# Perceiver block on one Trainium2 core: softmax sums laid on a masked square, one set of products for adding and broadcasting them

## The reference, cut to what matters

```
q = split_heads(layernorm(x) @ Wq.T + bq)       # x: 32 batches, 64 rows, 256 columns; 16 heads of 16
k = split_heads(ctx @ Wk.T + bk)                # ctx: 32 batches, 1601 keys, 256 columns
v = split_heads(ctx @ Wv.T + bv)
score = einsum('bhqd,bhkd->bhqk', q, k) * sqrt(16)
attn = softmax(score, axis=-1)
out = einsum('bhqk,bhkd->bhqd', attn, v)
x = x + out @ Wp.T + bp
x = x + circuit_block(layernorm(x))             # cosines, running products, a small two-layer network
x = x + experts(layernorm(x))                   # a shared expert and two of seven routed ones
```

## Time and profile before

| what | us |
|---|---|
| median of 3 runs (1733.7 to 1734.82) | 1734.32 |
| the profiled execution | 1735.91 |
| its span, first to last instruction | 1734.1 |
| attention, its 64 `weigh` blocks: first and last start | 83.9, 1209.1 |

### The profile page before, as it was taken

The page is one execution under the profiler, slowest core; times in us unless marked ns, Lnnn a source line. Parts: engine busy times, 40 slices in busy tenths (PEclk is TensorE's granted clock), DMA queues, the critical chain, the costliest instruction groups (busy, mean ns, idle before and its releaser), DMA issues. The chain is left out here.

```text
span 1734.1 us, 59228 instructions
## 1 busy us (share of the span) xinstructions
PE 1666.1 (96%) x24340; PEld 1377.8 (79%) x24340; DVE 1425.4 (82%) x3316; ACT 1220.5 (70%) x3297; POOL 948.8 (55%) x1427
## 2 busy tenths in 40 slices
PE   7999999999999999999999999996798899999998
PEld 4777777777777777777777777775577899999998
DVE  5699898998989989898998989888875676767657
ACT  3687788777888778887877878787554365656552
POOL 5265646556465565655556555554310448888850
PEclk9999999999999999999999999996797999999999
DMA  5011111211112111121111111111102356666632
GB/s 177 22 64 46 48 66 42 67 45 53 60 42 68 45 63 50 42 68 45 65 48 45 65 46 64 48 48 57 62 25 86 122 177 228 219 228 219 226 120 103
DMA packets 43439, 147.89 MB, mean 85 GB/s; under 512 B 5680, under 2 KB 25008, under 8 KB 39712
## 3 DMA queue, kind: packets, MB, share of 16 engines
q1 hardware_dynamic: 38416, 130.72, 22.1%
q0 software_dynamic: 4752, 13.38, 2.5%
HBM read 129.79 MB, written 14.16 MB: 83 GB/s over the span
## 5 line engine op out<-in xcount | busy, mean ns | idle before, releaser
L506 ACT ACTIVATE a_probs<-a_probs,a_bias 128x401 f32<-128x401 f32 x1024 | 631.8, 622 | 2.1
L721 DVE TENSOR_SCALAR_CACHE_REDUCE a_probs<-a_pss 128x401 f32<-128x401 f32 x1024 | 526.2, 570 | 56.9 <-PE a_pss L976 42.6
L736 DVE STREAM_TRANSPOSE a_pT<-a_probs 128x1664 f32<-128x1664 f32 x256 | 488.1, 1907 | 61.3 <-PE a_pso L1005 59.8
L976 PE MATMUL a_pss<-a_keys,a_qown 32*32 32x401 f32 x8192 | 273.6, 508 | 2.7 <-issue 1.3
L316 POOL TENSOR_TENSOR a_clo<-a_raw,a_chi 128x416 fp32r<-128x416 f32 x240 | 251.5, 1081 | 0.0
L1005 PEld LDWEIGHTS a_pso<-a_pT,a_v 128*32 128x32 f32 x6656 | 184.5, 112 | 45.7 <-issue 42.8
L1005 PE MATMUL a_pso<-a_pT,a_v 128*32 128x128 f32 x6656 | 202.5, 279 | 3.5 <-ACT a_op L521 2.7
L339 POOL TENSOR_SCALAR a_ex<-a_probs,a_marks 128x4 f32<-128x4 f32 x256 | 75.9, 296 | 220.2 <-ACT a_probs L506 218.1
L1670 PE MATMUL e_psg<-e_xh,e_guh 128*128 128x256 f32 x660 | 189.5, 287 | 5.5 <-DVE e_hl L1416 4.0
L506 ACT ACTIVATION_READ_ACCUMULATOR a_probs<-a_probs,a_bias 128x1 f32 x1024 | 194.5, 190 | 0.0
L1671 PE MATMUL e_psg<-e_xl,e_guh 128*128 128x256 f32 x660 | 186.6, 283 | 0.0
(11 more groups left out here) (253 smaller groups left out, 4288.8 us busy)
## 6 DMA issues: line engine op xcount, KB each, us to landing
a_raw<-in_ctxT SPq DMA_DIRECT2D x60, 832.0 KB, 4.4
f_gur<-in_wgu SPq DMA_DIRECT2D x24, 1408.0 KB, 6.2
f_dr<-in_wd SPq DMA_DIRECT2D x24, 768.0 KB, 4.7
e_big<-ys_scr SPq DMA_DIRECT2D x8, 512.0 KB, 7.0
a_probs<-in_ctxT SPq DMA_DIRECT2D x2, 1664.0 KB, 9.3
a_x<-in_x SPq DMA_DIRECT2D x16, 128.0 KB, 4.4
rows_scr<-f_a SPq DMA_DIRECT2D x8, 256.0 KB, 2.3
rows_scr<-f_a SPq DMA_DIRECT2D x4, 512.0 KB, 3.5
```

The lines of the kernel that those rows point to most:

```text
L506: nc.scalar.activation(z, z, ACT.Exp, bias=bias[:, h % 2, at_bias:at_bias + 1], scale=-1.0, accum_out=esum[:, h % 2, j, 2 * e + r:2 * e + ...
L721: nc.vector.tensor_scalar(probs[:, at % RING, j, 0:KG], ps_s[:, j, 0:KG], -SCALE, None, ALU.mult, ALU.min, accum_out=nmax[:, h % 2, at_max ...
L736: nc.vector.transpose(pT[:, turned_slot(h, i)].rearrange("p j k -> p (j k)"), probs[:, at % RING].rearrange("p j k -> p (j k)")).then_inc( ...
L976: mm = nc.tensor.matmul(ps_s[32 * g:32 * g + 32, j, 0:KG], q_own[32 * j:32 * j + 32, n % 2, m, e, 32 * r:32 * r + 32], keys[32 * j:32 * j ...
```

## The change

The keys are dealt out differently: key i goes to group i mod 4, so that group 0 has 401 real keys and the others 400 (`REAL`). The one absent column of groups 1 to 3 is set to -1e30 once in the score banks and never written again, so its probability is 0. With that `less_extra`, `total`, `spread_sums` and `spread` are gone, and the scale in the last value copy too. In their place POOL lays the 128 by 16 sums on a masked 128 by 512 square (`lay_sums`), PE adds them over all partitions and broadcasts them in one set of four products with a matrix of ones (`totals`, behind `weigh`), DVE takes the reciprocal of the broadcast 128 by 128 bank (`invert`), and ACT's `copy_out` becomes two activations of 64 columns with the parity as scale. On PE the lone first-quarter step of an even period joins the second quarter, and the two steps of the third quarter both stand ahead of `spread_max`. In DVE's order behind the loop the last `invert` stands behind `rows.0 scan.0`.

```diff
-        plan = [[(n + 1, 2)], [(n + 1, 3), (n + 1, 4)], [(n + 1, 5), (n + 1, 6)], [(n + 1, 7), (n + 1, 8), (n + 1, 9)]]
+        plan = [[], [(n + 1, 2), (n + 1, 3), (n + 1, 4)], [(n + 1, 5), (n + 1, 6)], [(n + 1, 7), (n + 1, 8), (n + 1, 9)]]
...
-            def spread_sums(h):
-
-                pool.wait_ge(inverse_ready, h + 1)
+            def lay_sums(h):
+
+                pool.wait_ge(exp_done, HALF * HALF * (h + 1))
                 if h > 0:
 
-                    pool.wait_ge(sums_filled, h)
+                    pool.wait_ge(totals_filled, h)
...
+                nc.gpsimd.tensor_tensor(out=sums_in[:].rearrange("p j (q b) -> p (j q) b", b=32),
+                                        in0=esum[:, h % 2].rearrange("p j q -> p (j q)").unsqueeze(2).to_broadcast([P, 4 * HALF, 32]),
+                                        in1=mark[:, DIAG].unsqueeze(1).to_broadcast([P, 4 * HALF, 32]), op=ALU.mult).then_inc(sums_laid, 1)
...
                 act.wait_ge(o_filled, h + 1)
-                act.wait_ge(sums_filled, h + 1)
+                act.wait_ge(inverse_ready, h + 1)
...
-                nc.scalar.copy(o_part[:, h % 2, :], ps_o[:, 0:2 * P]).then_inc(o_copied, 1)
+                for e in range(2):
+                    last = nc.scalar.activation(o_part[:, h % 2, SQ * e:SQ * (e + 1)], ps_o[:, SQ * e:SQ * (e + 1)], ACT.Identity, scale=mark[:, e:e + 1])
+                last.then_inc(o_copied, 1)
...
             def invert(h):
 
-                dve.wait_ge(total_filled, h + 1)
-                if h > 0:
-
-                    dve.wait_ge(sums_spread, h)
-                nc.vector.reciprocal(inverse[:], ps_s[0:32, 0, W:W + 4 * HALF]).then_inc(inverse_ready, 1)
+                dve.wait_ge(totals_filled, h + 1)
+                if h > 1:
+
+                    dve.wait_ge(o_scaled, h - 1)
+                nc.vector.reciprocal(o_part[:, h % 2, P:2 * P], ps_o[:, P:2 * P]).then_inc(inverse_ready, 1)
...
+            nc.vector.memset(ps_s[:, :, min(REAL):KG], ABSENT).then_inc(absent_set, 1)
...
                     if i == 2 and h > 0:
-                        if h + 1 < NH:
-                            dve.wait_ge(s_filled, HALF * (HALF * (h + 1) + 3) + 1)
                         invert(h - 1)
...
-            def spread(h):
-
-                pe.wait_ge(sums_spread, h + 1)
+            def totals(h):
+
+                pe.wait_ge(sums_laid, h + 1)
                 for j in range(HALF):
-                    for e in range(2):
-                        mm = nc.tensor.matmul(ps_o[32 * j:32 * j + 32, P + SQ * e:P + SQ * (e + 1)], mark[0:32, PARITY[e]],
-                                              sums_in[:, j, 2 * e:2 * e + 2].rearrange("p q b -> p (q b)"), start=True, stop=True)
-                mm.then_inc(sums_filled, 1)
+                    mm = nc.tensor.matmul(ps_o[32 * j:32 * j + 32, P:2 * P], ones[:], sums_in[:, j, :], start=True, stop=True)
+                mm.then_inc(totals_filled, 1)
...
                 if h > 0:
                     weigh(h - 1)
+                    totals(h - 1)
                 for z in steps[0]:
                     step(*z)
 
-                if h > 0:
-                    total(h - 1)
                 if h + 1 < NH:
                     scores(h + 1, 3)
...
-                for z in steps[2][:1]:
+                for z in steps[2]:
                     step(*z)
+
                 if h + 1 < NH:
                     spread_max(h + 1)
-                for z in steps[2][1:]:
-                    step(*z)
-
                 if h + 2 < NH:
                     scores(h + 2, 1)
-                if h > 0:
-                    spread(h - 1)
```

More of the change, by code:

```diff
@@ L39 @@
 RING, TURNED = 6, 5
-OWN, DIAG, EXTRA, KEPT, PARITY = slice(0, 2), slice(2, 34), slice(34, 35), slice(35, 36), (slice(36, 68), slice(68, 100))
+REAL = tuple((SK + QK - 1 - g) // QK for g in range(QK))
+ABSENT = -1e30
+OWN, DIAG = slice(0, 2), slice(2, 34)
 SCALE = float(HD) ** 0.5
@@ L154, in attention_and_circuit @@
         a_id_sb = sb("a_id", [P, P])
-        mark = sb("a_marks", [P, 100])
+        mark = sb("a_marks", [P, 34])
         tick = sb("a_tick", [P, 1])
         nmax, lowest, bias = sb("a_nmax", [P, 2, HALF * HALF]), sb("a_low", [HALF * HALF, 2, 32]), sb("a_bias", [P, 2, HALF * HALF])
-        esum, extra, sums = sb("a_esum", [P, 2, HALF, 4]), sb("a_ex", [P, HALF]), sb("a_sums", [P, 2, HALF, 4])
-        sums_in = sb("a_sin", [32, HALF, 4, 32])
-        inverse, o_part = sb("a_inv", [32, HALF * 4]), sb("a_op", [P, 2, 4 * SQ])
+        esum, sums_in, ones = sb("a_esum", [P, 2, HALF, 4]), sb("a_sin", [P, HALF, P]), sb("a_ones", [P, 32])
+        o_part = sb("a_op", [P, 2, 4 * SQ])
         oT = sb("a_oT", [P, NC, P])
@@ L372, in _ @@
             nc.gpsimd.memset(unset, 0.0).then_inc(cleared, 1)
+            nc.gpsimd.memset(ones[:], 1.0).then_inc(cleared, 1)
             nc.gpsimd.memset(tick[:], 0.0).then_inc(ticked, 1)
@@ L389, in period @@
                 n, k = h // 2, h % 2
+                if h > 0:
+                    lay_sums(h - 1)
                 if h > 1:
                     gather(h - 2)
-                less_extra(h, 0)
                 if h % 4 == 1 and h > 4:
@@ L437, in _ @@
             period(NH - 3)
+            lay_sums(NH - 3)
             gather(NH - 4)
-            less_extra(NH - 2, 0)
-            less_extra(NH - 2, 1)
             pool.wait_ge(kv_filled, STEPS * B)
             nc.gpsimd.memset(expo[:], -0.5).then_inc(expo_set, 1)
-            for i in range(0, NT // 2, 4):
+            for i in range(0, NT, 4):
                 nc.gpsimd.memset(heads[:, i:i + 4, :], 0.0).then_inc(zeroed, 1)
[L445 to L449, removed]
+            lay_sums(NH - 2)
             gather(NH - 3)
-            less_extra(NH - 1, 0)
             pool.wait_ge(by_set, 6)
@@ L462, in _ @@
             nc.gpsimd.memset(c[:].rearrange("p t (h d) -> p (t h) d", d=HD)[:, :, 0], 0.0).then_inc(zeroed, 1)
[L463 to L464 removed]
+            add_bias(NT - 1)
+            lay_sums(NH - 1)
             gather(NH - 2)
[L466 to L467 removed]
             pool.wait_ge(turned, HALF * NH)
@@ L502, in exponentials @@
                 act.wait_ge(bias_ready, h + 1)
+                if i == 0 and h > 1:
+                    act.wait_ge(sums_laid, h - 1)
                 for j in some:
@@ L542, in copy_steps @@
                         else:
-                            nc.scalar.activation(v_of(n)[:, t, :], step_bank(at)[:, 0:D], ACT.Identity, scale=mark[:, KEPT]).then_inc(kv_copied, 1)
+                            nc.scalar.copy(v_of(n)[:, t, :], step_bank(at)[:, 0:D]).then_inc(kv_copied, 1)
             def copy_rows(g):
@@ L969, in scores @@
                 if at == 0:
-                    pe.wait_ge(q_ready_all, NC * NG)
+                    pe.wait_ge(absent_set, 1)
                 for j in range(HALF):
@@ L975, in scores @@
                     for g in range(QK):
-                        mm = nc.tensor.matmul(ps_s[32 * g:32 * g + 32, j, 0:KG], q_own[32 * j:32 * j + 32, n % 2, m, e, 32 * r:32 * r + 32],
-                                              keys[32 * j:32 * j + 32, m, g * KG:(g + 1) * KG], start=True, stop=True)
+                        mm = nc.tensor.matmul(ps_s[32 * g:32 * g + 32, j, 0:REAL[g]], q_own[32 * j:32 * j + 32, n % 2, m, e, 32 * r:32 * r + 32],
+                                              keys[32 * j:32 * j + 32, m, g * KG:g * KG + REAL[g]], start=True, stop=True)
                     mm.then_inc(s_filled, 1)
@@ L1066, in _ @@
             pe.wait_ge(ctx0_split, NC)
-            pe.wait_ge(cleared, 3)
+            pe.wait_ge(cleared, 4)
             for s in range(FIRST_STEPS):
@@ L1125, in _ @@
                 if stage == "weigh":
-                    total(NH - 1)
                     weigh(NH - 1)
+                    totals(NH - 1)
                     pe.wait_ge(loaded, 16 * 7)
-                    idle_work(6)
-                    spread(NH - 1)
+                    idle_work(4)
                 elif stage == "project":
@@ L1796 @@
     ctx = a["ctx_1024"]
-    ctx = np.concatenate([ctx[:, :SK - 1].reshape(B, QK, KG - 1, D), np.broadcast_to(ctx[:, None, SK - 1:], (B, QK, 1, D))], axis=2)
-    ctx = np.pad(ctx, ((0, 0), (0, 0), (0, W - KG), (0, 0))).reshape(B, QK, KT, 32, D).transpose(0, 2, 1, 3, 4).reshape(B, SKP, D)
+    ctx = np.stack([np.pad(ctx[:, g::QK], ((0, 0), (0, W - REAL[g]), (0, 0))) for g in range(QK)], axis=1)
+    ctx = ctx.reshape(B, QK, KT, 32, D).transpose(0, 2, 1, 3, 4).reshape(B, SKP, D)
     at = np.arange(P)
```

35 lines of the change are left out of this document (6 added, 29 removed), and 2 rows, old and new, of the table DVE_ORDER.

## The result

| | before | after |
|---|---|---|
| median, us | 1734.01 (4 runs, 1733.5 to 1734.82) | 1758.38 (4 runs, 1756.82 to 1758.86) |
| span of the profiled execution | 1734.1 | 1757.0 |
| first `weigh` | 83.91 | 87.29 |
| first to last `weigh` | 1125.14 | 1144.59 |
| behind the last `weigh` | 525.07 | 525.14 |

The ratio is 1.0142, with a 95% interval from 1.0128 to 1.0156: slower by some 24 us. Of the 22.9 us by which the span grew, 3.4 lie ahead of the first `weigh` and 19.5 between the first and the last, where the odd periods grew and the even ones shrank.

A forecast was written before the change was run, and what follows sets the result against it. PE was taken to be the bound, in a loop with DVE that binds odd periods. 30 x (1.03 - 0.40) = +18.9 plus 2.7 for the last reciprocals gave +21.6 and 1756 us, range 1724 to 1771.

The forecast's parts named there:

- the predicted case: Reciprocal holds DVE from 0.8 to 1.3 us and ACT's copies hold PE; 1740 to 1769 us, chance 0.68.
- the predicted loop: `weigh` releases DVE's turn; reciprocal and third take then release PE's scores of quad 0, 7.95 + R behind `weigh`'s start.
- The reciprocal: On DVE, ahead of the third take: widened from 16 to 128 columns, 234 ns becomes 1.11 us, 7.8 ns a column.
- R: Time the reciprocal holds DVE before the next take: 1.09 us predicted, against 0.19 before the change.
- Eight plain passes a column: The skill page's reading of the reciprocal on DVE: 1.29 us, R = 1.27, whole forecast 1767.
- ACT's copies: Fourth quarter: PE waits for step copies after later `spread_max` (start s), 0.75 us in odd periods, 0.24 in even.
- `totals`: On PE behind `weigh`: eight more instructions than `weigh` alone, 0.24 us with the turn to the scores.
- Even periods: `weigh` to `weigh`: 17.98 us against 18.38, -0.40; only R above 0.87 shows, costing 0.22.
- Odd periods: `weigh` to `weigh`: the loop binds, 16.96 + R = 18.05 us against 17.02, +1.03.
- Periods with `project_out`: Every fourth period, treated as the other odd ones, so +1.03 us.
- The sum: 30 even and 30 odd periods give +18.9 us, the last three reciprocals 2.7; +21.6 in all.
- A sign that failed: DVE's wait for `weigh` ahead of its second turn was to become smaller than 0.94 us.

The follow-up runs named there:

- the late reciprocal: The changed kernel with DVE's reciprocal moved from ahead of the third take to behind the fourth, before the last turn: 1736.23 us.
- the copy: The changed kernel with a plain copy of the 128 by 128 bank in place of its reciprocal, the division left out: 1738.01 us.
- the kernel with the lone step back: The changed kernel with the lone step of even periods put back in the first quarter, behind `weigh` and `totals`: 1765.82 us.
- `spread_max` back: The changed kernel with `spread_max` put back between the two steps of the third quarter: 1726.04 us.
- both moves: The changed kernel with `spread_max` between the third quarter's steps and the reciprocal behind DVE's fourth take: 1711.59 us.

## Why the prediction was right

The forecast was 1756 for a measured 1758.4, in the predicted case, by the predicted loop. The two costs and where they fall were right; that the number came so close is luck, since several terms were off and made up for each other.

- **The reciprocal.** Mis-sized: 1.11 us and R = 1.09 were predicted, 924 ns and R = 0.85 measured. The 7.8 ns a column had put all of the excess of one narrow instruction on its columns. With three widths measured in the same place, 234 ns for 16 columns, 525 for 64 and 924 for 128, a column costs (924 - 525) / 64 = 6.2 ns from 64 to 128, and 5.4 times the plain 1.15. In the late place it is the same, (941 - 541) / 64. Eight plain passes a column are too many, as the prediction had read the repeat count of 8 in the Trainium skill ("VectorE: DVE Perf Modes", section "First, the fixed hardware budget") to get 1.29 us; the measurement decides.
- **The loop of odd periods.** Right in form: PE leaves the scores of quad 0 at 644.85 - 636.11 = 8.74 behind `weigh`, where 7.95 + 0.85 gives 8.80. Of that block's 1.85, 0.96 is waiting, a little short of the "over a microsecond" of the prediction.
- **ACT's copies.** Right in mechanism, too small in size: 0.75 predicted, 0.91 measured in an odd period (4.14 against 3.23), 0.24 predicted and 0.42 measured in an even one. `spread_max` at s = 647.91 let the copies land at s + 2.33 and s + 3.82, against 2.29 and 3.80. What was left out is PE's side: it starts 0.05 behind a landing, and each start after a wait costs 0.10 more, which the block behind shows (653.14 - 651.79 = 1.35, where the step without a wait takes 632.81 - 631.56 = 1.25).
- **`totals`.** Predicted 0.24, measured 639.33 - 636.11 = 3.22 for `weigh` and `totals`, against 2.86 for `weigh` alone: 0.36.
- **Even periods.** Predicted 17.98, measured 18.04. R is below the 0.87 from which it shows, so the 0.22 was not paid, and 0.12 for `totals` and 0.18 for ACT were.
- **Odd periods.** Predicted 18.05, measured 17.92: 0.24 less for R, 0.06 less in the loop, 0.16 more for ACT.
- **Periods with `project_out`.** Wrongly treated as the other odd ones: +1.12, not +0.91. DVE's residual there waits for `project_out`, which now stands behind `totals`: it starts 602.90 - 598.81 = 4.09 behind `weigh`, where it was 590.23 - 586.31 = 3.92, and the residual starts later by the same 0.17. So the loop holds another small piece. This DVE timeline of the changed kernel shows the wait:

```profile
604.14 0.42 DVE L726 TENSOR_TENSOR a_x<-a_psm,a_x 128x256 f32<-128x256 f32 x1 [0.24 <-PE a_psm L996]
```

- **The sum.** Up to the last four intervals, 59 of them, the `weigh` blocks lie 1079.97 - 1059.47 = 20.5 us further apart, where 18.9 was predicted. The last four take 64.62 instead of 65.67: a gain of 1.0 where 2.7 was to be paid for three reciprocals. In the kernel before, DVE waits there once for POOL's sums, the 2.8 us of the earlier trace rows; that wait is gone. The first `weigh` starts 3.4 later, which was not foreseen. 20.5 - 1.0 + 3.4 = 22.9 is the difference of the two spans.
- **A sign that failed.** DVE's wait ahead of its second turn did not shrink (0.96 for 0.94): the take ahead of that turn is itself released by PE's scores of quad 2 (636.26), so both ends of the wait hang on PE.

The start of the program is explained only in part. The first `weigh` starts at 87.29 in the changed kernel, at 87.42 with the late reciprocal, at 85.73 with the copy, and between 82.77 and 83.91 in all other kernels. Two pieces of the changed kernel's delay can be read. At 62.98 PE has waited 1.23 for ACT, behind the later extrema; the kernel with the lone step back has the same wait. In the period behind that (period 0, where the lone step has moved too) PE stops 0.72 for DVE in the scores of quad 3, ahead of which the lone step had stood, and then its granted clock falls. These are the stretches from 72 to 76 us of the changed kernel and of the one with the lone step back:

```profile
72.00:76.00 4.00, 4.00 (x15) 3.83 (x15) 3.96 (x10) 2.10 (x8) 0.00 (x0) 0.57 0.63 217
72.00:76.00 4.00, 4.00 (x56) 2.91 (x55) 4.00 (x11) 3.71 (x13) 0.00 (x0) 1.00 0.47 178
```

The third number from the end is PE's clock, 0.57 against 1.00 of the full 2.4 GHz; the lower level is 1.2 GHz. The two key steps there take 75.77 - 71.84 = 3.93, where the even period above takes 624.59 - 622.17 = 2.42 for two: 1.5 longer. With `spread_max` back PE makes the same stop of 0.72 and the clock stays full (1.00 from 68 to 76), so the stop alone does not bring the fall; with both moves it falls again (0.79). What brings it is open.

## What to carry to other kernels

Follow a wide operation to the queue where it stands: the same 0.9 us, 64 times, cost 22 us ahead of the take that the bottleneck waits for, and next to nothing behind the take after that, as long as the engine had room. Work that is taken off the bottleneck may have been the cover of another engine's delay: ask of each removed block what was catching up under it. Where two loops both nearly bind, gains do not add, so the second repair is measured on top of the first.

## What the runs showed that had not been expected

- A reciprocal of 128 partitions costs 6.2 ns a column from 64 to 128 columns, at either place in DVE's order (525 and 924 ns, 541 and 941 ns). Halving its columns gained 10.0 us in the old place and 4.9 in the late one.
- A product block that waits pays again on starting: 0.10 us for the six products of a key step, beyond the wait.
- `spread_max` and the scores behind it overlap: in PE's timeline of the odd period the two take 649.00 - 647.91 = 1.09 us in all, yet that is no less than 0.18 + 0.89 one after the other.
- On DVE a take behind a turn starts sooner in the changed kernel: from start to start 600.66 - 598.64 = 2.02 us before, 649.80 - 647.88 = 1.92 now. The take has lost a wait for POOL's sums, which may be the reason; no run tells it apart.
